# A graph layer's last gathers, its scatter waits and its third matmul layer rearranged

## The reference, cut to what matters

```python
h = relu(layernorm(x))                                  # all 100000 rows
t = silu(edge_radial @ W1 + b1); t = silu(t @ W2 + b2)  # 8 -> 64 -> 64 per edge
tpw = t @ W3 + b3                                       # 256 weights per edge: W00, W110, W01, W10, 8x8 each
hs_e, hv_e = h[src][:, :8], h[src][:, 8:].reshape(-1, 8, 3)
m0 = A * (einsum('eu,euw->ew', hs_e * sh0, W00) + C * einsum('eui,ei,euw->ew', hv_e, sh1, W110))
m1 = A * (einsum('eu,ei,euw->ewi', hs_e, sh1, W01) + einsum('eui,euw->ewi', hv_e * sh0, W10))
agg = segment_sum(concat([m0, m1]), dst) / 4
out = x + concat([hs @ Ws, einsum(hv, Wv)]) / sqrt(8) + agg
```

## Time and profile before

| | us |
|---|---|
| median of the runs (lowest to highest) | 618.04 (617.47 to 618.76) |
| profiled execution, its own time | 617.0 |
| its span, first to last instruction | 615.0 |
| busy: PE, DVE, ACT, POOL | 529.1, 463.4, 389.3, 488.3 |
| POOL: scatters (196), gathers (188) | 305.7, 181.6 |
| mean granted TensorE clock | 0.824 of full |

### The profile page before, as it was taken

How to read it: one execution, slowest core, us unless ns; L and a number is a source line. 1 busy time by engine, 2 the same in 40 slices (tenths; PEclk the granted TensorE clock), 3 DMA queues, 4 the chain that set the end, 5 groups by cost and what they waited for, 6 DMA issues and landing times.

```text
span 615.0 us, 12788 instructions
## 1 busy us (share of the span) xinstructions
PE 529.1 (86%) x2843; PEld 394.7 (64%) x2867; DVE 463.4 (75%) x1125; ACT 389.3 (63%) x1103; POOL 488.3 (79%) x393
## 2 busy tenths in 40 slices
PE   6979999999799999888897998889899999987700
PEld 4768888888556666656664766566565666654600
DVE  4678889898489997777787777768877788857700
ACT  3426565656477977767596757757785778776400
POOL 6777777777777888888888888888888787888787
PEclk9959999999697887777888777778877778787755
DMA  4756667664200122222222222222222222222222
GB/s 129 193 184 185 203 195 203 207 204 141 82 14 15 12 11 12 11 10 10 12 11 11 11 10 13 9 11 10 12 10 11 11 8 10 10 10 9 10 9 9
DMA packets 53524, 34.36 MB, mean 56 GB/s; under 512 B 37062, under 2 KB 40920, under 8 KB 53464
## 3 DMA queue, kind: packets, MB, share of 16 engines
q0 software_dynamic: 34240, 6.32, 18.0%
q1 hardware_dynamic: 12054, 14.60, 8.2%
q10 hardware_dynamic: 7170, 12.81, 5.7%
HBM read 17.59 MB, written 16.08 MB: 55 GB/s over the span
## 4 chain that ended last, share of the span: by engine, by line
POOL 64%; issue 21%; DMA 14%; POOLq 0%
POOL out_dram L325 38%; POOL xg L313 25%; DMA out_dram<-sums,idx_i 14%; DMA src_all<-in_src_dram 0%; POOLq L335 0%; POOLq L341 0%; POOLq L342 0%; POOLq L331 0%
## 5 line engine op out<-in xcount | busy, mean ns | idle before, releaser
L325 POOL DMA_INDIRECT out_dram<-sums,idx_i x196 | 305.7, 1560 | 65.6 <-issue 54.4
L313 POOL DMA_INDIRECT xg<-in_x_dram,src_all x188 | 181.6, 966 | 58.4 <-issue 57.0
L645 PE MATMUL ps<-w3blk,x 128*128 128x512 f32 x196 | 142.5, 819 | 1.6 <-issue 0.4
L692 PE MATMUL ps<-msg,eq 128*128 128x32 f32 (+1 forms) x980 | 124.7, 287 | 1.8 <-DVE msg L1014 1.8
L692 PEld LDWEIGHTS ps<-msg,eq 128*128 128x128 f32 x980 | 124.4, 207 | 2.1 <-DVE msg L1014 2.0
L994 DVE TENSOR_REDUCE red<-prod 128x128 f32<-128x1024 f32 x49 | 97.8, 1996 | 0.1
L476 ACT ACTIVATE dsq<-ps,dcol 128x512 f32<-128x512 f32 x196 | 87.1, 537 | 0.2 <-PE ps L657 0.2
L464 ACT ACTIVATE sums<-ps 128x132 f32<-128x132 f32 x49 | 13.7, 279 | 111.6 <-POOLq L335 87.7
L645 PEld LDWEIGHTS ps<-w3blk,x 128*128 128x128 f32 x196 | 46.9, 253 | 44.4 <-issue 40.8
L498 ACT ACTIVATE eq<-dsq,onecol 128x384 f32<-128x384 f32 x147 | 73.4, 519 | 0.0
L657 PEld LDWEIGHTS ps<-ident,dcol 128*128 128x128 f32 x196 | 25.4, 151 | 59.1 <-issue 57.0
(11 more groups left out here) (106 smaller groups left out, 803.9 us busy)
## 6 DMA issues: line engine op xcount, KB each, us to landing
xg<-in_x_dram SPq DMA_DIRECT2D x936, 0.1 KB
xin<-in_x_dram SPq DMA_DIRECT2D x48, 256.0 KB, 3.0
out_dram<-oc ACTq DMA_DIRECT2D x48, 256.0 KB, 2.3
out_dram<-sums,idx_i POOLq DMA_INDIRECT x196, 3.0
xg<-in_x_dram,src_all POOLq DMA_INDIRECT x188, 2.4
er_all<-in_edge_attr_dram SPq DMA_DIRECT2D x1, 780.0 KB
sh_all<-in_edge_attr_dram SPq DMA_DIRECT2D x1, 390.0 KB
xin<-in_x_dram SPq DMA_DIRECT2D x1, 192.0 KB, 3.1
```

The source lines that it names most:

```text
L313: pool.indirect_dma_start(xg[:, t * D:(t + 1) * D], None, x, bass.IndirectOffsetOnAxis(ap=src_all[:, t:t + 1], axis=0)).then_inc(signal, 16)
L325: pool.indirect_dma_start(out, bass.IndirectOffsetOnAxis(ap=idx_i[:, k % NS, a:a + 1], axis=0), sums[:, k % NS, a * DR:a * DR + D], None, ...
L645: pe.matmul(o, x2[:, k // 2 % 2, j * P:(j + 1) * P], w3blk[:, :], start=True, stop=False)
L692: m = pe.matmul(psSUM[:, a * DR:a * DR + n], eq[:, k % 2, o:o + P], msg[:, k % 2, b, 0:n], start=(b == a), stop=(b == a - 1 and (a < BT - ...
```

## The change

- POOL gathers tiles 0 to 185 (`G1` = 196 - 10), all before the first scatter; the gathers between the batches are gone, and tiles 186 to 195 are SP's (`RT` = 10).
- SP reads byte offsets from a new tile `row_at`, which DVE computes from the row numbers ahead of its node step 10; SP waits for that after chunk 12. A row is now a slice of 128 bytes of `x` seen as bytes. Seven rows follow each chunk.
- Late features come in three units, of 30, 36 and 10 tiles (`LATE_UNITS`). The first two are made in passes 0 to 2, the third in the last pass, where the wait for SP's rows and `feat_sum` now stand ahead of the products of its first batch. Passes 3 to 10 make none.
- The carry comes from tiles 0 and 1 of the batch before: tile 0's goes to tiles 2 and 3, tile 1's to tile 3. ACT makes `csq` and `ceq` 384 wide in two instructions each, and PE waits for the carry before tile 2 of the sum.
- So a tile may share rows with fewer of those in flight: tile 3 waits for tiles 3 and 2 of the batch before, tile 2 for tile 1, tile 1 for tile 0.
- `layer3` issues the bias first, then per tile two matmuls of 64 rows and 256 columns, one on partitions 0 to 63 and one on 64 to 127.

```diff
-    GT, GL, GA, RT = 10, 7, 157, 8
+    GT, RT = 10, 10
     G1 = T + 1 - RT
...
+    PASSES = NU // 2
+    LATE_UNITS = [range(GF, GF + 30), range(GF + 30, G1), range(G1, T + 1)]
...
-                            row_i[0:1, o:o + w], engines=[mybir.EngineType.SP], min_val=0, max_val=N - 1,
+                            row_at[0:1, o:o + w], engines=[mybir.EngineType.SP], min_val=0, max_val=(N - 1) * D * 4,
...
-                    sp.dma_start(xg[p:p + 1, t * D:(t + 1) * D], x[ds(nodes[p % 32], 1), :])\
+                    sp.dma_start(xg[p:p + 1, t * D:(t + 1) * D].bitcast(u8), x_bytes[:, ds(nodes[p % 32], D * 4)])\
...
                 if c == 12:
-                    sp.wait_ge(row_loaded, 16 * RT)
+                    sp.wait_ge(s["rows_at"], 2)
                 if 12 <= c < FULL:
-                    gather_rows(4)
+                    gather_rows(7)
...
-            for t in range(GA):
+            for t in range(G1):
                 gather(t)
...
                 if k != 0:
-                    pool.wait_ge(s["scattered"], q * 16 * (BT - 1))
-                tile(BT - 1, s["scattered"])
+                    pool.wait_ge(s["scattered"], q * 32)
+                tile(3, s["scattered"])
+                if k != 0:
+                    pool.wait_ge(s["scattered_next"], q * 16)
+                tile(2, s["scattered"])
                 if k != 0:
                     pool.wait_ge(s["scattered_last"], q * 16)
                 pool.nop(nofuse=True).then_inc(s["landed"], 1)
-                for a in range(BT - 2, 0, -1):
-                    tile(a, s["scattered"])
+                tile(1, s["scattered_next"])
                 tile(0, s["scattered_last"])
...
             for q in range(NQ):
-                if GA + q < G1:
-                    gather(GA + q)
                 scatter(q, q)
...
-                    act.activation(csq[:, :], psDT[:, BW - P:BW], ACT.Square, bias=dcol[:, (k - 1) % NS, 0:1], scale=-1.0)
+                    act.activation(csq[:, 0:2 * P], psDT[:, 2 * P:BW], ACT.Square, bias=dcol[:, (k - 1) % NS, 0:1], scale=-1.0)
+                    act.activation(csq[:, 2 * P:3 * P], psDT[:, 3 * P:BW], ACT.Square, bias=dcol[:, (k - 1) % NS, 1:2],
+                                   scale=-1.0)
...
-                    act.activation(ceq[:, k % 2, :], csq[:, :], ACT.Relu, bias=onecol[:, :], scale=-4.0,
-                                   accum_out=ccnt[:, (k - 1) % NS, :])
+                    for a, o in ((0, slice(0, 2 * P)), (1, slice(2 * P, 3 * P))):
+                        act.activation(ceq[:, k % 2, o], csq[:, o], ACT.Relu, bias=onecol[:, :], scale=-4.0,
+                                       accum_out=ccnt[:, (k - 1) % NS, a:a + 1])
...
                 for h in range(2):
-                    j = 2 * (k % 2) + h
-                    o = psTP[k % 2][:, h * 2 * NTP:(h + 1) * 2 * NTP]
-                    pe.matmul(o, x2[:, k // 2 % 2, j * P:(j + 1) * P], w3blk[:, :], start=True, stop=False)
-                    m = pe.matmul(o, ones3[:, :], b3rows[:, :], start=False, stop=True)
+                    pe.matmul(psTP[k % 2][:, h * 2 * NTP:(h + 1) * 2 * NTP], ones3[:, :], b3rows[:, :], start=True, stop=False)
+                for a in range(2):
+                    j = 2 * (k % 2) + a
+                    for h in range(2):
+                        half = slice(h * HR, (h + 1) * HR)
+                        m = pe.matmul(psTP[k % 2][:, (2 * h + a) * NTP:(2 * h + a + 1) * NTP],
+                                      x2[half, k // 2 % 2, j * P:(j + 1) * P], w3blk[half, h * NTP:(h + 1) * NTP],
+                                      start=False, stop=(a == 1))
                 m.then_inc(s["tp_ready"], 1)
...
                 for a in range(BT):
+                    carried = [] if k == 0 else [[], [], [(0, 0)], [(P, 0), (2 * P, 1)]][a]
+                    if a == 2 and k >= 1:
+                        pe.wait_ge(s["carry_done"], q)
                     for b in [a] + list(range(a)):
...
+                    for o, b in carried:
+                        m = pe.matmul(psSUM[:, a * DR:a * DR + D], ceq[:, k % 2, o:o + P], carry[:, (k - 1) % 2, b, :],
+                                      start=False, stop=(b == a - 2))
                 m.then_inc(s["sum_ready"], 1)
...
+                if c == 10:
+                    dve.wait_ge(s["rows_at"], 1)
+                    dve.wait_ge(row_loaded, 16 * RT)
+                    dve.tensor_scalar(row_at[:, :], row_i[:, :], float(D * 4), None, ALU.mult).then_inc(s["rows_at"], 1)
                 node_step(c)
...
+                        if last and h == 0 and r == 0:
+                            late_landed(scaled)
+                            feat_sum(scaled, *unit(scaled))
                         products(q, k, u)
```

More of the change, by code:

```diff
@@ L70, in gnn_layer @@
     GF = EARLY * GT
-    LATE = NU // 2 - 1
-    assert 0 <= GF + GL * LATE - (T + 1) <= 1
+    PASSES = NU // 2
+    LATE_UNITS = [range(GF, GF + 30), range(GF + 30, G1), range(G1, T + 1)]
+    LATE = len(LATE_UNITS)
+    GW = max(len(tiles) for tiles in LATE_UNITS)
     DR = D + 1
@@ L155, in gnn_layer @@
         lcnt = sb("lcnt", [P, NS, BT])
[L156 to L159, removed]
+        csq = sb("csq", [P, 3 * P])
+        ceq = sb("ceq", [P, 2, 3 * P])
+        ccnt = sb("ccnt", [P, NS, 2])
+        carry = sb("carry", [P, 2, 2, D])
         dmt_all = sb("dmt_all", [P, T + 1])
@@ L199, in gnn_layer @@
         gathered = [sem(f"gathered{i}") for i in range(EARLY)]
-        gathered_late = [sem(f"gathered_late{i}") for i in range(LATE)]
+        gathered_late = [sem(f"gathered_late{i}") for i in range(LATE - 1)]
         gathered_row = [sem(f"gathered_row{i}") for i in range(RT)]
@@ L257, in _ @@
                 for t in (2 * k, 2 * k + 1):
-                    sp.dma_start(w1big[t * NB:(t + 1) * NB, t // 2, (t % 2) * HR:(t % 2 + 1) * HR], W1)\
+                    pair, half = t // BT * 2 + t % 2, t % BT // 2
+                    sp.dma_start(w1big[t * NB:(t + 1) * NB, pair, half * HR:(half + 1) * HR], W1)\
                       .then_inc(s["w_loaded"], 16)
@@ L311, in gather @@
             def gather(t):
-                signal = gathered[t // GT] if t < GF else gathered_late[(t - GF) // GL]
+                signal = gathered[t // GT] if t < GF else gathered_late[int(t >= GF + 30)]
                 pool.indirect_dma_start(xg[:, t * D:(t + 1) * D], None, x,
@@ L512, in _, with edge_pass @@
             mlp_two(1, 1)
-            def edge_pass(v, first, last, squares):
-                n = EARLY + v
+            def edge_pass(v, first, last, roots=None, squares=None):
                 for h in range(2):
@@ L524, in edge_pass @@
                         copy_sums(q - 1, kq - 1)
+                    if h == 0 and last:
+                        feat_square(squares, width(squares))
                     dst_square(q + 1, kq + 1)
-                    if h == 0 and not last:
-                        feat_std(n - 1, GT if first else GL)
+                    if h == 0 and not last and roots is not None:
+                        feat_std(roots, width(roots))
                     if not end:
@@ L531, in edge_pass @@
                     dst_equal(q + 1, kq + 1)
[L532 to L535, removed]
+                    if h == 1 and not last and squares is not None:
+                        feat_square(squares, width(squares))
                     copy_sums(q, kq)
@@ L692, in sum_batch @@
                         m = pe.matmul(psSUM[:, a * DR:a * DR + n], eq[:, k % 2, o:o + P], msg[:, k % 2, b, 0:n],
[L693 to L699 removed]
+                                      start=(b == a), stop=(not carried and (b == a - 1 or a == 0)))
+                    for o, b in carried:
+                        m = pe.matmul(psSUM[:, a * DR:a * DR + D], ceq[:, k % 2, o:o + P], carry[:, (k - 1) % 2, b, :],
+                                      start=False, stop=(b == a - 2))
                 m.then_inc(s["sum_ready"], 1)
@@ L730, in edge_pass @@
                         layer2(u + 2, k + 2, 2 if last else 4)
-            for v in range(NU // 2):
-                edge_pass(v, v == 0, v == NU // 2 - 1)
+            for v in range(PASSES):
+                edge_pass(v, v == 0, v == PASSES - 1)
             sum_batch(NQ - 2, NQ - 2)
@@ L1055, in edge_pass @@
                         sum_vectors(q, k)
-                        if h == 1 and r == 0 and v < LATE - 1:
-                            feat_centre(n, t0, GL)
-                        if h == 0 and r == 0 and last:
-                            feat_centre(n - 1, was, GL)
+                        if h == 1 and r == 0 and centred is not None:
+                            feat_centre(centred, *unit(centred))
                         if ready:
                             index_later(q - 2, k - 2)
-                        if h == 0 and r == 0 and not last:
-                            feat_var(n - 1, ww)
+                        if scaling and r == 0 and not last:
```

(13 more changed lines are left out.)

97 lines of the change are left out of this document (51 added, 46 removed).

## The result

The changed kernel takes 612.2 us (median of four runs, 611.5 to 613.9) against 617.9 before: ratio 0.9905, 95% interval 0.9885 to 0.9925, faster by 5.7 us. The forecast was 607.6, its range 605 to 616. The direction and the main mechanism held; the gain is about half of the forecast one. 612.2 also lies outside the forecast's own 605 to 611: the stated range holds it only by the part that was added for rival B, and B is not what happened.

What follows compares the result with a forecast made beforehand. POOL was taken to bound the kernel: first scatter at 237.4, plus 195 pitches of 1.865 (363.7), plus 3.5 to the end, gives span 604.6, profile 606.6, median about 607.6; own range 605 to 611, stated range 605 to 616.

Steps and rivals of the forecast that it cites:

- rival B: Scatters on POOL: stalls stay in part as landings get longer when scatters are nearer together; about 612, chance 12%.
- POOL bounds, and goes on doing so: Whole span: POOL alone carries it, gathers then scatters; afterwards scatter pitch 1.86 to 1.87 throughout, computing engines held back by POOL.
- Gathers ahead, 4.4 us less: POOL: 28 more gathers before the first scatter (202.28 to 237.4), 30 between batches gone (39.6 us); net 4.4 us less.
- the cover: Early stretch: POOL's gathers up to 237.4 hide node phase, first four batches and DVE's new waits; 49 us.
- Scatter waits, 5.8 us: POOL's scatters: each tile waits for one issued three pitches (5.58 us) earlier, so stalls of 5.8 us go.
- Third layer, nothing: PE's third layer: 64-row pairs, overlapping or not, stay under 7.86 us a batch, so worth nothing.
- Slack of compute, 7.86 us a batch: Compute behind POOL: with a lead of 17.7 us over 44 batches it could run at 7.86 before POOL starves.
- SP's rows: the step that failed: SP's row DMAs: a byte offset needs neither register step, 0.33 us a row, rows done at 473.
- With one staying 0.40: SP's row DMAs: if one register step remains, a row costs 0.40 us and rows are done at 539.
- until 544 they cost nothing: Last pass: SP's rows may come until 544, as batch 42's indices need some 6.5 us and its scatter starts at 550.7.
- A: Last pass: SP's rows come late; at 0.477 us a row they land at 631, about 695 in all; chance 10%.
- C: Computing engines: compute becomes the bound, PE's third layers at 1.2 GHz, 8.3 us a batch; 627, chance 4%.

Runs made afterwards that it cites:

- before_waits: The kernel before with only the new scatter waits, the wider csq, ceq and carry, and PE's new sum: 617.0 us, ratio 0.9971.
- old_l3: The changed kernel with the third layer of before (one 128-row matmul of 512 columns per two tiles): 610.5 us, ratio 0.9895.
- before_pairs: The kernel before with only the third layer in 64-row pairs: 618.6 us, ratio 1.0013.
- rows_early: The changed kernel with DVE's conversion of the row numbers at node step 8 for 10, so SP may begin sooner: 607.6 us, ratio 0.9835.
- late_wait: The changed kernel with the wait for SP's rows and their features' sum and centring moved behind the messages of batch 44: 608.5 us, ratio 0.984.
- row_numbers: The changed kernel with SP taking row numbers and addressing rows of x in place of byte offsets: 718.8 us, ratio 1.1624.
- early_late_2: The changed kernel with DVE's conversion at step 8 and the wait for SP's rows behind batch 44's messages, undisturbed chip: 608.2 us, ratio 0.9839.

## Why the prediction was right, and where it was off

- *POOL bounds, and goes on doing so.* Right. Busy 80%, mean pitch 1.867 in the middle, lead 12.7 us or more from batch 9 to 41.
- *Gathers ahead, 4.4 us less.* The first scatter came at 239.2, not 237.4. A gather took 1.269 us on average from the first to the last (236.1/186), and 1.2608 before (199.2/158); I had used the clean pitch of 1.256 for the added ones, and the longest took 1.78 where the earlier trace rows has 1.19 at most. Cost: 1.7 us. That the node phase, the preamble and DVE's waits for late tiles cost nothing was right: up to 239 all of it is covered. When the early stretch was disturbed on one chip, the first scatter came 199 us behind the gathers and the change lost 44 us. The prediction said what the cover was but gave its loss no chance.
- *Scatter waits, 5.8 us.* The mechanism is shown: undone, it costs 14.7 us. But it is not a term that can be credited alone. before_waits got 1.1 of the 5.8, since compute could not follow 7.43 us with a unit of late features in every pass. The prediction counted the late features of three passes as nothing, hidden; before_waits beside old_l3 says that this is the edit that lets the waits pay, though no run makes that edit alone.
- *Third layer, nothing.* Right, shown twice (old_l3, before_pairs). Both matmuls of a pair do overlap: four of 256 columns take 1.13 us, one of 512 takes 1.08. So the Trainium skill's sentence on row groups (TensorE: Matmul & The Clock Gate, Part 3) agrees with the trace; of the drain at a change of mode (TensorEngine Tiling, Key Properties) no row shows more than 0.36 us of idle PE ahead of the bias and the pairs. The lower granted clock, which the prediction did not foresee, takes part of that back.
- *Slack of compute, 7.86 us a batch.* Right in size (a lead of 16 to 17 us at best), but compute used a part of it: 13 us at batches 16 and 24.
- *SP's rows: the step that failed.* "I take 0.33 ... with 70 us to spare." Measured 0.397, the case "With one staying 0.40", and the last row issued at 538.7, which that case gave as 539. I took the lower end because nothing seemed to need the MOVE; the row was there and said one per DMA.
- *"until 544 they cost nothing"* failed too. I had followed the wait to the next batch's indices (6.5 us said, 6.3 measured) and assumed that the batches behind it would come at POOL's pace. The chain through PE's half-finished sum, ACT's queue and DVE's second and third wait takes 29.4 us to batch 44. From 544 to that batch's scatter the prediction had left 21.6; from the measured landing, 540.1, POOL's own pace left 28.2, and batch 44 came 1.2 us late, batch 46 another 1.6. rows_early and late_wait show that either repair takes this away. The rule I had written myself (what is queued behind the waiting instruction, and who waits for that) was applied to the first hidden wait and not to this one.
- *The rivals.* A's mechanism is what cost the 2.8 us, by a late row, but under A's own threshold of 544; row_numbers shows its full size. B did not happen: the longest landing after is 4.5 us for 4.4 before, under the 5.58 that each tile now has. C did not either: up to batch 41 compute keeps 12.7 us of lead. That 612.2 is also B's figure is chance.

The sum: 1.7 (gathers) + 4.2 (scatters: 2.8 idle, 1.05 one long scatter, 1.3 in small ones, less 1.0 because the median pitch is 1.86 for 1.865) + 0.1 at the end = 6.0, for 6.1 us between the predicted span of 604.6 and the measured 610.7. The medians are only 4.6 apart (612.2 for 607.6), because the profiled run after is 0.3 us above its median and 0.2 less lies around its span, while the prediction had added 1.0 for a profiled run below its median. With the last pass repaired the sum holds but for the gathers: in early_late_2 the first scatter comes at 239.44, 195 pitches take 363.5 for 363.7, and the span is 606.4.

## What to carry to other kernels

Follow a wait past its first victim: an engine that stops in the middle of an accumulation holds a second, and that one the first again; count until the leads are back. When a bound engine gets faster, edits that "cost nothing" elsewhere become what pays for it, so parts timed alone do not add up (1.1 us here for a part that is worth 14.7 in the whole). And a table of leads, consumer's start less producer's, shows in one line what a releaser in brackets can hide.

## What the runs showed of the hardware

- A DMA from SP whose source is a register's byte offset needs one MOVE (29 ns); a row number needs a FUSED_REGOPS (37 ns) too. With the gaps this is 0.478 (row_numbers) against 0.397 us a row (after), with 2.1 us for every 32 register loads included.
- Pairs of 64-row fp32 matmuls on the two halves of the array overlap: eight records in 1.13 us. A kernel with them is granted a lower mean clock: 0.762 to 0.783 for 0.818 to 0.836 (before_pairs and before), 0.798 to 0.818 for 0.842 to 0.853 (after and old_l3).
- POOL's sequencer runs far ahead: it passed the first batch's signal at 188.1 while gathers ran until 202; where a scatter did wait for a landing, it started 0.74 us behind it.
